# Four changes in one step of a two-layer image kernel: leaky unit folded into matmuls, shorter roots, pixels turned by DMA, moments on VectorE

## The reference, cut to what matters

```
# layer 0, mixer, on layernormed pixels: every 3x3 patch (9 pixels j, 96 channels) on its own
y        = <pixel j, w_mask[v]> / (|pixel j| * |w_mask[v]|)      # v = 0..511
v*, j*   = argmax of y over v and j;  s = y[v*, j*]
inp      = concat(s * pixel[j*] + (1 - s) * w_mask[v*],  y[v*, 0..8])   # 96 + 9 values
h        = leaky_relu(inp @ w_i1.T + b_i1, 0.2)       # 288
vcs      = tanh(h @ w_i2.T + b_i2)                     # 96
conv_out = w_conv applied to (relu(vcs @ w_l1.T + b_l1) @ w_l2.T + b_l2)
x1 = x + conv_out
x2 = x1 + FFN0(layernorm(x1))
# layer 1, mixer: z = layernorm(x2); response normalisation over 5x5 pixels
x3 = x2 + z / (2 + 1e-4 * box5x5(sum over channels of z*z)) ** 0.75
x4 = x3 + FFN1(layernorm(x3))
# FFN: linear 96->384, relu, linear 384->96; operands rounded to fp8 (5 exponent
# bits, 2 mantissa bits), sums to fp16
```

## Time and profile before

| | |
|---|---|
| median of 3 runs | 3665.52 us (3658.46 to 3670.87) |
| the profiled execution, its own time | 3659.15 us |
| its span, first to last instruction | 3657.4 us |
| TensorE's mean granted clock | 0.945 |
| busy share of PE / DVE / ACT / POOL | 83% / 85% / 79% / 70% |

### The profile page before, as it was taken

The page is one execution under the profiler, slowest core; times in us unless marked ns, Lnnn a source line. Parts: engine busy times, 40 slices in busy tenths (PEclk is TensorE's granted clock), DMA queues, the critical chain, the costliest instruction groups (busy, mean ns, idle before and its releaser), DMA issues. The chain is left out here.

```text
span 3657.4 us, 63346 instructions
## 1 busy us (share of the span) xinstructions
PE 3038.1 (83%) x17928; PEld 1674.1 (46%) x17928; DVE 3093.2 (85%) x11127; ACT 2890.6 (79%) x7558; POOL 2569.9 (70%) x3993
## 2 busy tenths in 40 slices
PE   5887888888888888888888888888888888888755
PEld 2444454444445444444444444444444444444332
DVE  6788989889888998889889888889998888999631
ACT  0444888878788887878878788888888888888877
POOL 2455677767777777777767777776777777777753
PEclk9999999999999999999999999999999999999855
DMA  3111111111111121111111111121211111111000
GB/s 84 45 37 45 46 60 54 60 50 56 58 55 60 50 65 50 57 58 55 60 50 57 58 55 55 55 65 50 60 55 56 59 50 61 54 59 46 23 30 34
DMA packets 64515, 195.70 MB, mean 54 GB/s; under 512 B 11392, under 2 KB 14633, under 8 KB 64169
## 3 DMA queue, kind: packets, MB, share of 16 engines
q1 hardware_dynamic: 53928, 172.76, 14.8%
q0 software_dynamic: 10240, 18.89, 2.1%
HBM read 134.60 MB, written 57.02 MB: 52 GB/s over the span
## 5 line engine op out<-in xcount | busy, mean ns | idle before, releaser
L385 PE MATMUL banks<-wcT,xc 128*128 128x512 f32 x2304 | 1217.4, 631 | 108.8 <-DVE mx L731 104.2
L518 ACT ACTIVATE ffn_hid<-banks 128x384 f16<-128x384 f32 x2304 | 1026.8, 487 | 296.5 <-PE banks L362 273.1
L731 DVE TENSOR_REDUCE mx<-banks 128x1 f32<-128x512 f32 x1152 | 774.7, 683 | 227.9 <-PE banks L385 218.4
L362 PE MATMUL banks<-ffn_xT,w1q 128*128 128x384 bf16 x2304 | 678.1, 348 | 177.4 <-ACT ffn_hid L518 138.3
L994 POOL TENSOR_TENSOR ffn_f<-ffn_y,b2q 128x864 f16<-128x864 f16 x256 | 469.7, 1835 | 375.5 <-DVE nb L717 300.1
L362 PEld LDWEIGHTS banks<-ffn_xT,w1q 128*128 128x128 bf16 x2304 | 228.7, 100 | 790.6 <-ACT ffn_hid L518 588.1
L385 PEld LDWEIGHTS banks<-wcT,xc 128*128 128x128 f32 x2304 | 422.6, 199 | 350.8 <-DVE mx L731 150.8
L817 DVE TENSOR_SCALAR ffn_hid<-ffn_hid,b1q 128x1152 f16<-128x1152 f16 x768 | 420.9, 559 | 126.1 <-ACT ffn_hid L518 126.0
L996 POOL TENSOR_TENSOR x<-x,ffn_f 128x864 f32<-128x864 f32 x256 | 488.3, 1907 | 20.1
L551 ACT ACTIVATE ffn_x<-x,cols 128x96 fp8e5<-128x96 f32 x1152 | 461.4, 456 | 0.0
L551 ACT ACTIVATE ffn_x<-x,nb,roots 128x96 fp8e5<-128x96 f32 x1152 | 424.9, 455 | 0.0
(11 more groups left out here) (147 smaller groups left out, 4474.0 us busy)
## 6 DMA issues: line engine op xcount, KB each, us to landing
xt<-x_tok_in SPq DMA_DIRECT2D x128, 432.0 KB, 3.2
xc<-x_chan_in SPq DMA_DIRECT2D x128, 432.0 KB, 3.6
out_tok<-x SPq DMA_DIRECT2D x128, 432.0 KB, 2.5
win<-x_tok_in,xrow POOLq DMA_INDIRECT x128, 2.6
wrow<-vector_table,vidx POOLq DMA_INDIRECT x128, 2.7
shift<-shift_in SPq DMA_DIRECT2D x1, 960.0 KB, 5.7
vector_table<-wtab SPq DMA_DIRECT2D x1, 384.0 KB, 3.3
w1raw<-w_in SPq DMA_DIRECT2D x1, 288.0 KB, 6.4
```

The source lines that it names most:

```text
L362: last = pe.matmul(bank[:, 0:GW], w1q[:, ffn.layer, c * P:(c + 1) * P], ffn.xT[:, g * GW:(g + 1) * GW], start=True, stop=True)
L385: last = pe.matmul(ps_score[score_bank(j)], xc[p][:, j, :], wcT[:, :], start=True, stop=True)
L518: return nc.scalar.activation(dst, src, ACT.Copy)
L731: nc.vector.tensor_reduce(mx[p][:, j:j + 1], ps_score[score_bank(j)], AX.X, ALU.max).then_inc(score_taken, 1)
```

## The change

Four parts, in one diff:

1. The leaky unit. leaky(z) = 0.2 z + relu(0.8 z). ACT writes `h` = relu(0.8 z) straight from PSUM in one instruction (the bias is now a 106th row of `wi1`, against a column of ones in `inp`); the linear share goes through one more matmul of `inpT` with a product `leak` = 0.2 (w_i2 w_i1), made once. `z1` and DVE's `leaky` are gone.
2. Roots of eight links: a seed, a first round of four with a polynomial, a second of three. `win_vector` has no MAX8: `select` sums the picked column of `pix` (mean, maximum, root) into `chosen`, and the index is searched by the maximum that is there.
3. `norm` writes fp8 pixels in pairs; `turn` on SP issues a transposing DMA per FFN and step (16-bit elements, 5 blocks of 128 by 128), and PE reads the pairs as its moving operand in units of 512, 512 and 128 columns. PE's transposes and ACT's `xT` copies are gone. DVE rounds all three channel groups in one instruction.
4. Moments on DVE: seven instructions at the end of a step, between and behind `select`'s. POOL only copies one row per tile for the image. FFN 0's norm moves on ACT into thirds early in the step, the response normalisation's pixels move back.

```diff
+D1 = C + J + 1
-UNITS = G + HC * G + 2
+UNITS = HC * G + 2
+COLUMNS = [(0, 512), (512, 1024), (1024, J * P)]
 # SP
+            def turn(ffn, tile):
+                sp.wait_ge(ffn.x8_ready, tile + 1)
+                wait_past(sp, ffn.filled, tile * UNITS)
+                sp.dma_start_transpose(ffn.xT[:, :, :], ffn.x8[:].rearrange("p a c t -> p (a c t)").bitcast(F16)
+                                       ).then_inc(ffn.turned, 16)
+                if k.rear is not None:
+                    turn(ffn1, k.rear)
                 if k.fs is not None:
                     load_tokens(k.fs, k.p)
                     load_pixels(k.fs, k.p)
+                if k.back is not None:
+                    turn(ffn0, k.back)
 # PE
+                pe.matmul(ps_a[0:C, 0:P], leak[:, :], inpT[:, :], start=True, stop=False)
-                if k.rear is not None:
-                    fill(ffn1, k.rear, 0, G)
-                scores(6, 7)
-                if k.back is not None:
-                    fill(ffn0, k.back, 0, G)
+                scores(6, 8)
                 hidden_units(ffn0, k.back, 0, 2)
-                scores(7, 8)
+                scores(8, J)
                 hidden_units(ffn0, k.back, 2, 2)
 # ACT
+                    nc.scalar.activation(h[:].rearrange("c m p -> c (m p)"), ps_b[0:C, 0:M1 * P], ACT.Relu,
+                                         scale=1.0 - LEAK).then_inc(h_ready, 1)
+                norm0(k, 0, 3)
                 take_hidden(ffn1, k.rear, 0, 2)
 ...
+                norm0(k, 3, 6)
                 take_hidden(ffn1, k.rear, 2, 2)
 ...
+                norm0(k, 6, J)
                 take_hidden(ffn1, k.rear, 4, 2)
+                lrn_pixels(k, 1, 3)
                 take_hidden(ffn1, k.rear, 6, 3)
-                    norm(ffn0, x1[k.p], roots[k.p][:, 0, :], nb1)
+                lrn_pixels(k, 3, XA)
                 norm1(k, 0, 3)
-                if k.back is not None:
-                    take(ffn0, k.back, 0, G)
 # DVE
-            root_links = 11
+            root_links = 8
+            def moments(tile, p):
+                dve.wait_ge(stats_ready, tile + 1)
+                mc.add(nc.vector.tensor_tensor(d, of(1), of(4), ALU.subtract),
+                       nc.vector.tensor_tensor(m2, of(2), of(5), ALU.add))
+                yield
+                mc.wait()
+                mc.add(nc.vector.tensor_tensor(d, d, d, ALU.mult))
+                yield
+                mc.add(nc.vector.tensor_tensor(twice[p], of(1), of(4), ALU.add))
+                yield
+                mc.wait()
+                mc.add(nc.vector.scalar_tensor_tensor(out=ssq[p], in0=d, scalar=C / 4.0, in1=m2, ...))
+                yield
+                mc.wait()
+                mc.add(nc.vector.scalar_tensor_tensor(out=args[:, 0:3, :], in0=ssq[p], ...),
+                       nc.vector.tensor_copy(args[:, 3, :], ssq[p][:, 1, :]))
+                yield
-                f2c.add(nc.vector.max(vtop[:, :], ps_score[0]))
-                    round_up(c - 1)
+                nc.vector.tensor_scalar(bits, bits, TO_E5M2, TO_E5M2, ALU.add,
+                                        ALU.subtract).then_inc(ffn.hid_ready, 1)
                     mlp_input(k.f3, k.p, between)
+                scores(0, 2)
                 run(between)
-                scores(0, 2)
-                if k.f3 is not None:
-                    leaky(k.f3)
                 scores(2, WIN_TURN)
-                between = select(k.f1, k.p) if k.f1 is not None else iter(())
+                between = chain(select(k.f1, k.p) if k.f1 is not None else (),
+                                moments(k.stats, k.q) if k.stats is not None else ())
                 if k.back is not None:
                     hidden(ffn0, k.back, between)
                 run(between)
```

More of the change, by code:

```diff
@@ L20 @@
 from contextlib import ExitStack
+from itertools import chain
 import numpy as np
@@ L151, in build @@
         pow_half = sb("pow_half", [P, V // P])
-        half, c24, inv_c = (sb(n, [P, 3, J]) for n in ("half", "quarter_c", "inverse_c"))
         eps = sb("eps", [P, 3, J])
@@ L273, in __init__ @@
                 self.p = known % 2
+                self.tail_p, self.back_p, self.rear_p = ((known + PARTS[x]) % 2 for x in ("tail", "back", "rear"))
                 self.q = 1 - self.p
@@ L527, in _, with take @@
                 last = copy(wc[0:LH + q, q, 5 * C:J * C], banks[0:LH + q, 2 + 2 * q, 0:4 * C])
-            last.then_inc(w_act, 1)
-            def take(ffn, tile, first, units):
+            nc.scalar.activation(leak[:, :], banks[0:D1, 5, 0:C], ACT.Copy, scale=LEAK).then_inc(w_act, 1)
+            def take(ffn, tile, tp, first, units):
                 for u in range(first, first + units):
                     act.wait_ge(ffn.filled, tile * UNITS + u + 1)
-                    bank = banks[:, ffn.bank + u % 2, :]
-                    if u < G:
-                        last = copy(ffn.xT[0:C, u * GW:(u + 1) * GW], bank[0:C, 0:GW])
-                    elif u < G + HC * G:
-                        c, g = divmod(u - G, G)
-                        last = copy(ffn.hid[:, c, g * GW:(g + 1) * GW], bank[:, 0:GW])
+                    bank = banks[:, ffn.bank + (tp + u) % 2, :]
+                    if u < HC * G:
+                        c, g = divmod(u, G)
+                        c0, c1 = COLUMNS[g]
+                        last = copy(ffn.hid[:, c, c0:c1], bank[:, 0:c1 - c0])
                     else:
@@ L576, in norm1, with norm0 @@
                     act.wait_ge(x3_rest_ready, k.pre + 1)
-                norm(ffn1, x3[:, k.pre3], cols[k.q][:, 2, :], cols[k.q][:, 3, :], j0, j1)
+                norm(ffn1, k.pre, x3[:, k.pre3], cols[k.q][:, 2, :], cols[k.q][:, 3, :], j0, j1)
+            def norm0(k, j0, j1):
+                if k.back is None:
+                    return
+                if j0 == 0:
+                    act.wait_ge(root_ready, k.moments + 1)
+                    act.wait_ge(x1_ready, k.back + 1)
+                norm(ffn0, k.back, x1[k.p], roots[k.p][:, 0, :], nb1, j0, j1)
             def body(k):
@@ L581, in take_hidden @@
                     if tile is not None:
-                        take(ffn, tile, G + first, units)
+                        take(ffn, tile, k.back_p if ffn is ffn0 else k.rear_p, first, units)
                 if k.tail is not None:
-                    take(ffn0, k.tail, G + HC * G, 2)
-                lrn_pixels(k, 0, 1)
+                    take(ffn0, k.tail, k.tail_p, HC * G, 2)
                 if k.f3 is not None:
@@ L648, in _ @@
             nc.vector.memset(st3[:], 0.0)
+            for c in chosen:
+                nc.vector.memset(c[:], 0.0)
             nc.vector.memset(h1[:], 1.0)
+            nc.vector.memset(inp[:], 1.0)
             nc.vector.memset(wc[:], 0.0)
-            for operand in (*xc, wcT, winT, w1q, ffn0.xT, ffn1.xT):
+            for ffn in (ffn0, ffn1):
+                nc.vector.memset(ffn.x8[:].rearrange("p a c t -> p (a c t)").bitcast(U16), 0)
+            for operand in (*xc, wcT, winT, w1q):
                 last = nc.vector.memset(operand[C:P], 0.0)
@@ L1002, in tile_columns @@
                 wait_past(pool, ffn1.x8_ready, k.columns - 1)
-                for i in range(4):
-                    last = nc.gpsimd.tensor_copy(cols[k.p][:, i, :], cols_i[i][:, k.columns & SLOTS - 1, :])
-                last.then_inc(cols_ready, 1)
+                nc.gpsimd.tensor_copy(cols[k.p][:, :, :], cols_i[:, :, k.columns_slot, :]).then_inc(cols_ready, 1)
             def lrn_rest(k):
@@ L1085, in body @@
                     tile_columns(k)
-                if k.stats is not None:
-                    moments(k.stats, k.q)
                 if k.f1 is not None:
```

293 lines of the change are left out of this document (134 added, 159 removed).

## The result

The changed kernel takes 3802.2 us (median of 4 runs, 3797.9 to 3804.1), the kernel before 3666.7 (3658.5 to 3670.9): a ratio of 1.037, with a 95% interval of 1.035 to 1.039. It is slower by 3.7%, where 3825 us had been forecast. The profiled execution has a span of 3799.1 us at a mean granted clock of 0.923, against 3657.4 at 0.945.

What follows compares the result with a forecast made beforehand. A ring of dependent work across DVE, PE and ACT, no engine full, bounds the kernel. From 3659.15 us, +151 (ordinary steps), -16 (factors' steps) and +26 (drain) give 3820, median forecast 3825; range 3740 to 3930.

Steps and rivals of the forecast that it cites:

- The mechanism of the ordinary step: Walk from one `dots` to the next through roots, `conv`, scores and FFN 0: 26.7 us instead of 25.36.
- tail: Small DVE links of `select` and the moments between FFN 0's rounding and the next `dots`: 1.8 us, before 0.22.
- the signs named: Trace signs of a right forecast, among them PE idle 1.5 to 2 us for `inp` and moments right ahead of `dots`.
- ACT's wait for nb1: Ordinary step: ACT idle before its first FFN 0 norm pixel until the end of the roots' chain, at 4.9 us.
- DVE's wait ahead of the maximum of score 5: Ordinary step: DVE is there by 14.8 us and waits 1.7 us for PE's score 5.
- Factors' step: Step in which DVE also makes the response normalisation's factors: 30.5 us instead of 31.46, -1.0 each, 16 of them.
- Drain: The chain that ended last: +2.0 us a step for the DMA, +0.15 for the longer rounding; twelve steps, +26.
- The mis-sized term: Landing time of the transposing DMA, which moves 160 KB: taken as 4 us.
- half-clock step: Step with TensorE at 1.2 instead of 2.4 GHz for a part: 27.02 us, 1.66 above an ordinary one; left unchanged.
- The sum: Whole execution: 112 ordinary steps +151 us, 16 factors' steps -16, drain +26; +161, giving 3820.
- The rival "DVE's work sets the step": Faster case: `conv` begins by 11 us and a step takes 24.3 us, 3510 for the median; chance 0.25.
- the ring: Closed chain setting a step: `inp`, small network, `conv`, scores, DVE's maxima, FFN 0's hidden values, `select`, next `inp`.

Runs made afterwards that it cites:

- e1: The changed kernel with the moments back on GpSimd as nine instructions; 1.001 of the time of the kernel before.
- e3: The changed kernel with the links of the selection and the moments issued in pairs, one of each at a time; 0.9997 of the time of the kernel before.
- e9: The changed kernel with two more links in the roots' chain, each multiplying the roots by one; 1.042 of the time of the kernel before.
- e5: e3 with FFN 0's hidden units in the old order, units 0 and 1 behind score 6; 0.985 of the time of the kernel before.
- e7: e5 with most of FFN 0's LayerNorm moved behind FFN 1's hidden copies on ScalarE; 0.983 of the time of the kernel before.
- e11: e10 with FFN 0's rounding in two instructions, the first two blocks ahead of the third relu; 0.981 of the time of the kernel before.
- e8: The kernel before with the folded leaking unit and nothing else; 0.998 of the time of the kernel before.
- e2: The changed kernel with FFN 0's LayerNorm in one piece behind FFN 1's last hidden copy; 1.033 of the time of the kernel before.
- e10: The changed kernel with moments on GpSimd, and the late LayerNorm and old unit order of e7; 1.003 of the time of the kernel before.

## Why the prediction was right, and where it was not

**The mechanism of the ordinary step held.** Forecast against measured, from the start of `dots`: `inp` 1.9 and 1.72; maxima 0 and 1 until 3.0 and 2.92; roots 4.9 and 4.61; `conv` 12.5 and 12.29; maximum 5 at 16.5 and 16.30; first relu of FFN 0 at 21.7 and 21.43; rounding's end 25.0 and 24.83; tail 1.8 and 1.61; step 26.7 and 26.44. e1 and e3 show the moments' place as the cause (-1.1 and -0.95), e9 that in a step of 26.44 the roots are on the way (0.44 for 0.46). The forecast of +1.35 was +1.08; 0.2 of the difference is the tail. Of the signs named, PE's wait ahead of `inp` is 1.31 where 1.5 to 2 was said; ACT's wait for nb1 and the moments right ahead of `dots` are there.

**DVE's wait ahead of the maximum of score 5** was forecast at 1.7 and is 0.66. DVE came at 15.6 and not at 14.8, mostly since FFN 1's three relus took 2.51 us where they were 1.5; see the last section. In this step it cost nothing, because PE's score released the maximum.

**Factors' step: the sign was wrong.** I took -1.0 and it is +1.84. The step that failed is the one that let DVE's saved work and the wait for score 5 take 2.3 us off what this step has over an ordinary one: 3.8 was forecast, it was 6.10 and is 6.93 (33.37 less 26.44). DVE's busy time didn't fall, 29.44 us against 29.45. The wait that was to take up 1.7 is 0.66 in the ordinary step. And I never walked FFN 0 in this step. Its units 0 and 1, moved behind score 7, wait for DVE here, and DVE then waits for their copies ahead of its relus:

```profile
2370.32 0.52 DVE L871 TENSOR_SCALAR ffn_hid<-ffn_hid,b1q 128x1152 f16<-128x1152 f16 x1 [0.32 <-ACT ffn_hid L542]
...
2371.89 0.52 DVE L871 TENSOR_SCALAR ffn_hid<-ffn_hid,b1q 128x1152 f16<-128x1152 f16 x1 [0.97 <-ACT ffn_hid L542]
```

The unit order is worth 1.26 in this step and 0.44 in a plain one (e5), so 0.82 of the excess. The moments' tail is as long as in every step (33.65 less e3's 32.71 is 0.94) and was in the sum. The wait (1.04 too high) and the unit order leave 1.3 of the 3.1 us open. In the sum the factors' steps were -16 us and are +25.8, 42 us.

**Drain: +26 forecast, +3.7 measured.** Two rounds of the chain that ended last:

```profile
3734.99 1.54 ACT ffn_x L575 x4
3736.54 2.56 DMA ffn_xT<-ffn_x
...
3749.29 1.54 ACT ffn_x L575 x4
```

A round is 14.30 us, and was 13.50: +0.80 instead of +2.15. The mis-sized term is the transposing DMA, 2.56 instead of 4. That term is 1.44 smaller, where the round missed 1.35. There are ten such rounds and not twelve, +8.9 us in sum, and the four before them, in which other parts still drain, got 6.1 shorter; I had left them as they were. The Trainium skill's two pages differed on this: VectorE: DVE Perf Modes, "The three transpose paths", with 1309 ns for one block, an estimated 6.5 us for five in a row, and Advanced Engine Details and Errata, "X-Bar Transpose (TRN2)", which has them as fast as regular DMAs. The 2.56 us stand beside 2.6 for a plain load of 163.1 KB: the second holds.

**The clock.** The mean granted clock went from 0.945 to 0.923. For the plain steps this cost little: their mean is 0.44 above an ordinary step and was 0.43 above one. It was at work in the starting steps instead, 24.15 us at 0.93, where the kernel before has this:

```profile
137.87:161.52 23.65, 18.86 (x92) 9.70 (x92) 20.41 (x80) 11.85 (x31) 13.34 (x21) 1.00 0.15 45
```

I had taken the starting steps for ordinary ones. With the clock at 1.00 such a step would be an estimated 22.6 (e3's 21.53 and the tail of 1.06), 1.0 less than before; it is 0.5 more.

My reading of the clock in the kernel before was wrong as well. The stretch of 27.02 us that I took for a half-clock step is a step in which PE sums the windows (155 matmuls against 137), and it ends ahead of the next `dots`, which comes after 28.32. Such steps take 27.01 without a half-clock stretch too, 27.19 on the mean, and make 0.23 of the 0.55 us that I put down to the clock. That a plain step with a clock below 1.00 takes 27.03 on the median, so that 1.66 was the right price, is luck.

**The sum.** +161 forecast for the execution, +142 measured: the other 112 steps 42 us too high (18 of it the starting steps), the factors' steps 42 too low, the drain 22 too high, and 3.7 ahead of the first `dots` that I had not counted. The direction and the mechanism of the plain steps were right. That the sum came within 0.6% is luck: its errors cancel.

**The rival "DVE's work sets the step"** was near to what this change could have been. Once the tail is paired and the LayerNorm off the way, a step is 24.8 us, with DVE busy for 22.9 of it, and in e7 with the transposing DMA as a second limit. e7 and e11 are faster than both kernels, than the one before by 1.7 and 1.9%. What the shorter roots and the transposing DMA are worth by themselves no run shows: only the folded unit was put alone into the kernel before (e8).

## What to carry to other kernels

Where a chain of small dependent instructions is moved to a busier engine, ask what stands behind its last link, not how many instructions it has: here 1.1 us of moments at the end of the ring were the whole loss of an ordinary step, and issued in turn with a second chain they left the step 0.13 us above the one before. A saving that lies beside the ring shows nothing while the ring is as long: the folded unit took 1.20 us from DVE and left the time as it was. A transfer that is hidden is hidden by the order around it: moving its source later or its reader earlier brought it back as 0.6 to 1.5 us of waiting (e2, e7, e11). Walk every kind of step, since an order of units that is harmless in the ordinary one stood 5 us behind another engine in every eighth.

## What the runs showed of the hardware

VectorE's 16-bit relus can stand still while GpSimd works on a tensor. In the kernel before, in its factors' step, VectorE and then GpSimd:

```profile
2274.49 2.27 DVE L817 TENSOR_SCALAR ffn_hid<-ffn_hid,b1q 128x1152 f16<-128x1152 f16 x1
...
2277.80 0.51 DVE L817 TENSOR_SCALAR ffn_hid<-ffn_hid,b1q 128x1152 f16<-128x1152 f16 x1
```
```profile
2274.41 2.03 POOL L984 TENSOR_TENSOR prod_dot<-xt,wrow 128x864 f32<-128x864 f32 x1 [1.78 <-DMA wrow<-vector_table,vidx]
```

The same relu takes 2.27 us when it begins 0.08 behind GpSimd's product and 0.51 on the median; it ends 0.32 behind the product's end. Of 768 relus 25 take over 0.7 us in the kernel before, each beside a tensor instruction of GpSimd, and 184 in the changed one, all but one so. The Trainium skill, SBUF — State Buffer, "SBUF: two separate sides", says of the pair of ports that both engines use that it is locked for a whole instruction and not shared. The trace agrees for these, and the other way round: where a relu of the changed kernel begins within 0.05 us of one of GpSimd's response pixels (31 times), the relu takes 0.5 and GpSimd's instruction 1.19 where most take 0.83 to 0.92. It doesn't cover all: 77 relus of the kernel before begin 0.5 behind such an instruction, still inside its record, and take 0.5. For the changed kernel it is why FFN 1's three relus take 2.51 us in sum: they are beside GpSimd's response pixels. The wait is counted as busy time, so no sum of busy times tells that it can come or go with the order.

An indirect gather that went out together with a 432 KB load was usable 4.4 us after GpSimd had issued it (e10); in the changed kernel the median from issue to landing is 2.6 us. And with the transposing DMA the packets went from 64,515 to 236,605; the tokens' load went from a median of 3.2 to 3.8 us. In the changed kernel DVE waits for it twice (5.7 us in all, before once, 5.1), in e3 18 times (15.6 us).
